# A PSUM bank per tile and chunk from a table, 32x32 score tiles, and a new hand-written order of all steps, in an attention and FP4 feed-forward block

## The chip, the cores and the metric

The kernel runs on one core of a Trainium2 chip. Its engines are TensorE (PE, with its weight loads listed apart as PEld), VectorE (DVE), ScalarE (ACT), GpSimd (POOL) and SyncE (SP, which issues transfers). The metric is the device time of one execution in microseconds, the median of several.

## The reference, cut to what matters

A sequence of 2048 tokens of width 128 goes through a retention layer with 8 heads (16 wide for q and k, 32 for v), then a gated feed-forward layer (352 wide) whose inputs and weights are rounded blockwise to FP4. Each of the two is followed by a residual sum and a layer norm.

```python
q, k, v = x @ Wq, x @ Wk, x @ Wv            # q and k are rotated (rope)
decay  = where(diff >= 0, exp2(diff * s[head]), 0)
scores = einsum('bhqd,bhkd,hqk->bhqk', q * DQK ** -0.5, k, decay)
o = einsum('bhqk,bhkd->bhqd', scores, v)
o = o * rsqrt(mean(o * o) + EPS) * g_norm_w * silu(x @ Wg)
x = layernorm(x + o @ Wo)
h = silu(fp4_linear(x, w_gate)) * fp4_linear(x, w_up)
x = layernorm(x + fp4_linear(h, w_down))
```

`fp4_linear` divides each block of 16 by a sixth of its largest absolute value, rounds to the FP4 grid, scales back, and multiplies.

## The kernel before, in words

The tokens are worked through in 16 chunks of 128 (`C`), each of two half chunks of 64 (`CH`). All matmuls are in float32. A matmul of the program is two passes on TensorE (a transpose is one), so `scores` with 8 matmuls has 16 records a chunk. The retention runs over half chunks: a state `S` carries what came before, and a masked product of q and k covers the half chunk itself.

The steps of one chunk, by engine:

- PE: `project_qk`, `project_vg`, `transpose_qk`, `state_product` (k times v, tile `U`), `scores` (k times q, tile `sc`), `from_state` (q times S, opens tile `oT`), `values` (adds probs times v to `oT`), `transpose_o`, `transpose_y`, `out_projection` (tile `att`), `transpose_xq`, `gate`, `up`, `transpose_h`, `down`.
- DVE: `rotate` (rope products), `mask_scores`, `next_state` twice, `mean_square`, `gated`, `ln1_eps`, five steps of quantization of x and five of h (`amax`, `inv`, `ratio`, `plus`, `grid`), `h_product`, `ln2_sum`.
- ACT: the copies out of PSUM, SiLU, squares for the norms, the norms themselves, and `magic` of the quantization.
- POOL: `rotate_add`, reciprocal roots (`rms_rstd`, `ln1_rstd`, `ln2_rstd`), `gated_output`, `x_value`, `h_value`.

Before chunk 0 is through, the feed-forward weights are quantized too (`weights_...` on DVE and ACT) and transposed on PE.

Each engine has its own list of calls, written out by hand for the whole kernel, and works it off in that order; the engines meet in semaphores. The lists are a software pipeline: near the middle, PE works on `scores(8)`, `out_projection(6)`, `gate(4)` and `project_qk(12)` in one stretch.

PSUM has 8 banks. A table `BANKS` gives each kind of tile one bank (`sc` and `oT` four, `U` two), the same for all chunks. Before a step of PE writes a bank, `occupy` calls `free`, which waits until the reader of that bank's last tile is done. In the kernel before, it waits for as many readings as tiles of that kind have been filled.

The scores of one chunk are 8 matmuls: 4 pairs of heads, each in its own 32 rows of the array, times 2 half chunks of 64 keys, each in its own 64 columns of the array. In `from_state` a matmul takes 32 rows and 32 columns, in `state_product` and `values` 64 rows and 32 columns.

Of the kernel before, what the change touches and what calls it, by code (L numbers as in the profile page):

```python
# [7 lines left out]
H = 128  # L8
NH = 8
DQK = H // NH  # L10
VD = 2 * H
DV = VD // NH
I = 352
IP = 384
C = 128
# [59 lines left out]
def seq_postln_kernel(nc, x, xt, wqk, wvg, wo_g, w_gate_up, w_down, tab, cst, out):  # L75
# [4 lines left out]
    with ExitStack() as ctx:  # L80
# [3 lines left out]
        def sem(name):  # L84
# [79 lines left out]
        bank = lambda name: ps[:, BANKS[name][0], :]  # L164
        sc_ps = lambda j: ps[:, BANKS["sc"][j], 0:C]
        all_sc_ps = ps[:, 0:4, 0:C]
        oT_ps = ps[:, 0:4, 0:CH]
        oT_bank = lambda half, a: ps[:, BANKS["oT"][2 * half + a], 0:CH]
        o_ps = bank("o")[:, 0:VD]
        yT_ps = bank("yT")[:, 0:VD]  # L170
        qk_ps = bank("qk")[:, 0:256]
        qkT_ps = bank("qkT")[:, 0:256]
        vg_ps = bank("vg")[:, :]
        att_ps = bank("att")[:, 0:H]
        gate_ps = bank("gate")[:, 0:I]
        xqT_ps = bank("xqT")[:, 0:C]
        hT_ps = bank("hT")[:, 0:384]
        up_ps = bank("up")[:, 0:I]
        down_ps = bank("down")[:, 0:H]
        U_ps = lambda a: ps[:, BANKS["U"][a], 0:2 * DV]  # L180
        wg_T_ps, wu_T_ps = ps[:, 3, 0:I], ps[:, 2, 0:I]
        wd_T_ps = ps[:, 5, 0:384]
# [62 lines left out]
        def _(pe_engine):  # L245
# [5 lines left out]

            def free(n):
                name = tile.get(n)
                if name == "sc":
                    pe.wait_ge(mask_v, filled[name])
                elif name == "qk":
                    pe.wait_ge(rope_v, filled[name])
                elif name == "qkT":
                    pe.wait_ge(qe_act, filled[name])
                    pe.wait_ge(kT_act, filled[name])  # L260
                    pe.wait_ge(qo_act, filled[name])
                elif name == "vg":
                    pe.wait_ge(v_act, filled[name])
                    pe.wait_ge(silu_g_act, filled[name])
                elif name == "oT":
                    pe.wait_ge(oT_act, filled[name])
                elif name == "o":
                    pe.wait_ge(gate_v, filled[name])
# [671 lines left out]
```

## Time and profile before

| | |
|---|---|
| median of 3 runs | 133.45 us (133.18 to 134.6) |
| the profiled execution | 132.9 us, of which its span, first to last instruction, is 131.2 us |
| mean granted TensorE clock | 0.992 |
| busy | PE 119.2 us, DVE 110.0, ACT 88.8, POOL 87.7 |

The page gives busy time from first start to last end of each instruction, and matmuls overlap in the pipeline. What a PE step costs the next one is therefore better read from the distance between their starts in the timeline.

### The profile page before, as it was taken

Reading aid. Unit: us, or ns where it says so; the run is one execution under the profiler, and the core shown is the slowest. Engines: PE = TensorE matmul, PEld = TensorE weight load, DVE = VectorE, ACT = ScalarE, POOL = GpSimd, SP = SyncE. Lnnn points to the kernel's source line nnn. Section 1 sums busy time; section 2 is a strip of 40 time slices with the busy share of each in tenths; the row PEclk is TensorE's granted clock in tenths of the full one; section 3 lists DMA queues with packets and bytes.
Section 4 is the critical chain, followed back from the end, with each engine's and each line's share of the span. In section 5 each row is a group of like instructions: output and inputs, shape, how many; then the busy total and the mean of one; then the engine's idle time right before and its main releaser. Section 6 shows DMA issues by size and latency. Waiting matters only on the chain.

```text
span 131.2 us, 5084 instructions
## 1 busy us (share of the span) xinstructions
PE 119.2 (91%) x2040; PEld 82.7 (63%) x2040; DVE 110.0 (84%) x329; ACT 88.8 (68%) x311; POOL 87.7 (67%) x124
## 2 busy tenths in 40 slices
PE   4859699989999999999999999899999999999860
PEld 4425257766667676766675576567696788887650
DVE  1249999689589999999999998899999999999810
ACT  3143847557674776839576858778696878898882
POOL 5202726577687849784783869476949797996781
PEclk9999999999999999999999999999999999999996
DMA  3899991000000000000000000000000000011222
GB/s 104 256 273 392 425 440 45 5 5 5 0 5 0 5 0 5 0 7 0 5 2 5 0 5 2 5 0 5 0 5 0 25 2 0 20 40 30 58 80 80
DMA packets 4791, 7.68 MB, mean 59 GB/s; under 512 B 800, under 2 KB 3872, under 8 KB 4512
## 3 DMA queue, kind: packets, MB, share of 16 engines
q1 hardware_dynamic: 3744, 6.60, 14.3%
q10 hardware_dynamic: 1024, 0.76, 1.8%
q8 instruction: 16, 0.26, 0.9%
q14 instruction: 7, 0.06, 0.2%
HBM read 6.31 MB, written 1.05 MB: 56 GB/s over the span
## 4 chain that ended last, share of the span: by engine, by line
PE 66%; DVE 16%; DMA 6%; issue 4%; ACT 3%; POOL 2%; SPq 1%; POOLq 0%; DVEq 0%
PE ps L313 7%; PE ps L441 7%; DMA tabs_sb<-rope_tables 6%; PE ps L421 6%; PE ps L427 6%; PE ps L330 5%; PE ps L307 4%; PE ps L355 4%; PE ps L365 4%; DVE probs L727 3%; PE ps L433 3%; PE ps L386 3%; PE ps L341 3%; PE ps L388 2%; PE ps L387 2%
## 5 line engine op out<-in xcount | busy, mean ns | idle before, releaser
L859 POOL TENSOR_TENSOR rstd_h<-ms,minus_half 128x8 f32<-128x8 f32 x16 | 26.8, 1672 | 6.9 <-DVE ms L743 6.8
L313 PE MATMUL ps<-w_vg,xT_sb 128*128 128x512 f32 x32 | 17.4, 625 | 1.5 <-DVE S L738 1.1
L854 POOL TENSOR_TENSOR qk<-rope 128x256 f32<-128x256 f32 x16 | 11.7, 729 | 9.7 <-DVE rope L721 9.7
L878 POOL TENSOR_TENSOR xq<-x_ratio,xs 128x128 f32<-128x128 f32 x16 | 7.8, 489 | 11.9 <-DVE x_ratio L656 11.9
L441 PE MATMUL ps<-wd_T,hT 128*128 128x128 f32 x96 | 14.1, 283 | 1.3 <-DVE r L757 0.7
L721 DVE TENSOR_TENSOR rope<-ps,tabs_sb 128x512 f32<-128x512 f32 x16 | 11.0, 687 | 4.6 <-DMA tabs_sb<-rope_tables 3.3
L870 POOL TENSOR_TENSOR rstd<-veps,minus_half 128x1 f32<-128x1 f32 x16 | 9.3, 579 | 7.7 <-DVE veps L752 7.7
L886 POOL TENSOR_TENSOR hq<-h_ratio,hs 128x352 f32<-128x352 f32 x16 | 13.0, 815 | 1.7 <-DVE h_ratio L656 1.4
L441 PEld LDWEIGHTS ps<-wd_T,hT 128*128 128x128 f32 x96 | 12.1, 191 | 3.1 <-ACT hT L483 1.5
L727 DVE TENSOR_TENSOR probs<-ps,causal 128x512 f32<-128x512 f32 x16 | 11.0, 690 | 2.8 <-PE ps L330 2.4
L421 PE MATMUL ps<-wgu_T,xqT 128*128 128x352 f32 x32 | 13.3, 496 | 0.0
L483 ACT ACTIVATE oT<-ps 128x256 f32<-128x256 f32 x16 | 6.1, 382 | 9.9 <-PE ps L365 9.8
L427 PE MATMUL ps<-wgu_T,xqT 128*128 128x352 f32 x32 | 12.2, 464 | 0.0
L307 PE MATMUL ps<-w_qk,xT_sb 128*128 128x256 f32 x32 | 10.8, 421 | 1.0 <-DMA xT_sb<-x_transposed 1.0
L864 POOL TENSOR_TENSOR y<-gate_o,rstd_h 128x256 f32<-128x256 f32 x16 | 10.4, 651 | 0.5
L484 ACT ACTIVATE q_eo<-ps,consts 128x128 f32<-128x128 f32 x32 | 10.7, 376 | 0.0
L738 DVE SCALAR_TENSOR_TENSOR S<-S,consts,ps 128x64 f32<-128x64 f32 x31 | 8.3, 269 | 2.6 <-PE ps L341 2.2
L874 POOL TENSOR_TENSOR rstd<-veps,minus_half 128x1 f32<-128x1 f32 x16 | 9.1, 579 | 1.5 <-ACT r_sq L580 1.5
L483 ACT ACTIVATE v_sb<-ps 128x256 f32<-128x256 f32 x16 | 6.3, 391 | 5.0 <-PE ps L313 5.0
L561 ACT ACTIVATE silu_h<-ps 128x352 f32<-128x352 f32 x16 | 7.4, 463 | 2.8 <-PE ps L421 2.5
L501 ACT ACTIVATE h_magic<-h_ratio 128x352 bf16<-128x352 f32 x16 | 7.9, 496 | 1.5 <-DVE h_ratio L647 1.4
L483 ACT ACTIVATE hT<-ps 128x384 f32<-128x384 f32 x16 | 7.8, 487 | 1.6 <-PE ps L433 1.6
(110 smaller groups left out, 340.1 us busy)
## 6 DMA issues: line engine op xcount, KB each, us to landing
tabs_sb<-rope_tables SPq DMA_DIRECT2D x1, 2048.0 KB, 12.0
tabs_sb<-rope_tables SPq DMA_DIRECT2D x1, 1280.0 KB, 8.1
out<-x SPq DMA_DIRECT2D x16, 64.0 KB, 1.5
tabs_sb<-rope_tables SPq DMA_DIRECT2D x1, 512.0 KB, 4.6
xT_sb<-x_transposed SPq DMA_DIRECT2D x1, 512.0 KB, 7.6
xT_sb<-x_transposed SPq DMA_DIRECT2D x1, 320.0 KB, 5.5
tabs_sb<-rope_tables SPq DMA_DIRECT2D x1, 256.0 KB, 3.6
w_vg<-in_w_vg ACTq DMA_DIRECT2D x1, 256.0 KB, 3.9
```

Of the source, the lines that this page charges most:

```text
L307: mm(qk_ps, xT(c), w_qk[:], start=True, stop=True).then_inc(qk_pe, 1)
L313: mm(vg_ps, xT(c), w_vg[:], start=True, stop=True).then_inc(vg_pe, 1)
L421: mm(gate_ps, xqT[:, c % D, :], wgu_T[:, 0:I], start=True, stop=True).then_inc(gate_pe, 1)
L427: mm(up_ps, xqT[:, c % D, :], wgu_T[:, I:2 * I], start=True, stop=True).then_inc(up_pe, 1)
L441: last = mm(down_ps, hT[:, c % D, t, :], wd_T[:, t, :], start=t == 0, stop=t == 2)
L483: copy = lambda o, i: nc.scalar.activation(o, i, ACT.Copy)
L484: scaled = lambda o, i, by: nc.scalar.activation(o, i, ACT.Identity, scale=by)
L721: vec.tensor_tensor(rope[:, c % D, :, :], qk_ps.unsqueeze(1).to_broadcast([128, 2, 256]), tabs(c).rearrange("p (t n) -> p t n", t=2), ALU. ...
L727: vec.tensor_tensor(probs[:, c % D, :, :].rearrange("p (j e) q -> p j e q", e=2), all_sc_ps.rearrange("p j (e q) -> p j e q", e=2), causal ...
L854: gp.tensor_tensor(g16(qk[:, c % D, :]), g16(rope[:, c % D, 0, :]), g16(rope[:, c % D, 1, :])[:, :, ::-1, :], ALU.add).then_inc(qk_p, 1)
L859: gp.tensor_tensor(rstd_h[:, c, :], ms[:, c, :], minus_half[:], ALU.pow).then_inc(rms_p, 1)
L886: gp.tensor_tensor(hq[:, c % D, 0:I].rearrange("p (n k) -> p n k", k=BLK), h_ratio[:, c % 6, :].rearrange("p (n k) -> p n k", k=BLK), hs[: ...
```

## The change

1. Banks. `BANKS` now has an entry for each kind and chunk, so that for example `down` uses banks 7, 7, 3, 7, 5, ... instead of always 6. `sc` and `oT` keep banks 0 to 3 in every chunk. Each bank remembers which tile, and which count of it, it holds, and `free` waits for that count alone.
2. Scores. The 8 matmuls of 32 rows by 64 columns become 16 of 32 by 32 with the same 128 moving columns each.
3. Orders. The lists of PE, ACT, DVE and POOL are all rewritten. The calls are the same, but for a second `warm_up(4)` on PE (4 matmuls on an identity) between `project_qk(0)` and `project_vg(0)`. Most calls move by less than four places.
4. One added wait: `h_ratio_` of chunk 6 and later waits on DVE for `h_value` of six chunks before, which is the last reader of the buffer it writes.

```diff
-        BANKS = {"sc": (0, 1, 2, 3), "oT": (0, 1, 2, 3), "o": (1,), "yT": (7,), "qk": (4,), "qkT": (0,),
-                 "vg": (6,), "att": (5,), "xqT": (2,), "gate": (4,), "hT": (3,), "up": (7,),
-                 "down": (6,), "U": (6, 7)}
+        BANKS = {
+            "sc": (0, 0, 0, 0, 0, 0, 0, 0, 0, 0, 0, 0, 0, 0, 0, 0),
+            "oT": (0, 0, 0, 0, 0, 0, 0, 0, 0, 0, 0, 0, 0, 0, 0, 0),
+            "o": (2, 1, 1, 3, 3, 0, 2, 3, 2, 0, 0, 1, 0, 2, 1, 3),
+            "yT": (3, 4, 7, 6, 3, 3, 0, 0, 2, 7, 4, 4, 3, 4, 6, 6),
+            "qk": (5, 6, 6, 4, 6, 4, 4, 4, 4, 4, 4, 4, 4, 1, 4, 2),
+            "qkT": (2, 3, 2, 3, 2, 0, 2, 1, 2, 1, 3, 3, 3, 2, 0, 4),
+            "vg": (4, 4, 7, 5, 7, 6, 4, 6, 6, 6, 6, 6, 6, 6, 6, 6),
+            "att": (5, 5, 5, 5, 5, 5, 5, 5, 5, 5, 5, 5, 5, 5, 4, 0),
+            "xqT": (5, 6, 1, 5, 1, 5, 4, 6, 4, 4, 4, 6, 6, 6, 6, 6),
+            "gate": (4, 4, 4, 4, 4, 4, 4, 4, 4, 4, 4, 4, 2, 5, 5, 5),
+            "hT": (7, 7, 4, 0, 0, 1, 3, 7, 4, 7, 0, 3, 2, 3, 7, 7),
+            "up": (7, 7, 7, 7, 7, 7, 4, 7, 1, 1, 2, 6, 1, 2, 2, 2),
+            "down": (7, 7, 3, 7, 5, 7, 1, 7, 3, 4, 6, 5, 0, 5, 3, 3),
...
+            def banks(name, c):
+                b = BANKS[name][c]
+                return b if name == "U" else range(b, b + BANKS_OF.get(name, 1))
...
             def occupy(name, banks):
+                filled[name] += 1
                 for n in banks:
                     free(n)
-                    tile[n] = name
-                filled[name] += 1
+                    tile[n] = name, filled[name]
...
-                for a in range(2):
+                for k in range(4):
                     for j in range(NP):
-                        rows, keys = slice(32 * j, 32 * j + 32), slice(CH * a, CH * a + CH)
-                        last = mm(sc_ps(j)[keys, :], kT[rows, c % D, keys],
-                                  q_eo[rows, c % D, a, :, :].rearrange("p e q -> p (e q)"), start=True, stop=True)
+                        rows, keys = slice(32 * j, 32 * j + 32), slice(32 * k, 32 * k + 32)
+                        last = mm(sc_ps(c, j)[keys, :], kT[rows, c % D, keys],
+                                  q_eo[rows, c % D, k // 2, :, :].rearrange("p e q -> p (e q)"), start=True, stop=True)
...
-            def h_ratio_(c): quant_ratio(h(c), sh(c), blocks(h_ratio[:, c % 6, :]), hquant_v, c)
+            def h_ratio_(c):
+                if c >= 6:
+                    dve.wait_ge(hq_p, c - 5)
+                quant_ratio(h(c), sh(c), blocks(h_ratio[:, c % 6, :]), hquant_v, c)
```

The head of the orders of PE and DVE, before and after:

```diff
-            warm_up(4); project_qk(0); project_vg(0); transpose_qk(0); project_qk(1); state_product(0); scores(0)
-            project_vg(1); from_state(0); values(0); state_product(1); project_qk(2); transpose_qk(1); transpose_o(0)
+            warm_up(4); project_qk(0); warm_up(4); project_vg(0); transpose_qk(0); state_product(0); scores(0)
+            project_vg(1); project_qk(1); from_state(0); values(0); project_qk(2); transpose_o(0); state_product(1)
...
-            rotate(0); weights_amax(0); next_state(0, 0); next_state(0, 1); rotate(1); mask_scores(0); weights_inv(0)
-            weights_amax(1); weights_ratio(0); next_state(1, 0); rotate(2); next_state(1, 1); mean_square(0)
+            rotate(0); weights_amax(0); next_state(0, 0); weights_inv(0); next_state(0, 1); mask_scores(0)
+            weights_ratio(0); rotate(1); weights_amax(1); weights_inv(1); rotate(2); next_state(1, 0); mean_square(0)
```

A stretch of PE's order in the middle, and the end of the orders of PE and DVE:

```diff
-            out_projection(6); from_state(8); state_product(9); values(8); gate(4); transpose_qk(9); transpose_o(8)
-            transpose_y(7); project_vg(10); project_qk(12); transpose_xq(5); up(4); scores(9); out_projection(7)
+            transpose_xq(4); up(3); scores(8); out_projection(6); from_state(8); state_product(9); values(8); gate(4)
+            transpose_o(8); transpose_qk(9); project_vg(10); transpose_y(7); project_qk(12); up(4); transpose_xq(5)
+            scores(9); out_projection(7); from_state(9); state_product(10); values(9); gate(5); transpose_o(9)
...
-            transpose_xq(14); down(7); gate(14); transpose_h(9); up(14); down(8); transpose_h(10); transpose_xq(15)
-            down(9); up(15); gate(15); transpose_h(11); down(10); transpose_h(12); down(11); transpose_h(13); down(12)
+            down(6); transpose_h(8); transpose_xq(14); down(7); gate(14); up(14); down(8); transpose_h(9)
+            transpose_xq(15); transpose_h(10); gate(15); down(9); up(15); transpose_h(11); down(10); transpose_h(12)
...
-            h_plus_(13); h_ratio_(14); ln2_sum(9); h_grid_(13); h_plus_(14); h_product(15); ln2_sum(10); h_grid_(14)
-            h_amax(15); ln2_sum(11); h_inv(15); h_ratio_(15); ln2_sum(12); h_plus_(15); h_grid_(15); ln2_sum(13)
+            h_inv(14); h_plus_(13); h_ratio_(14); h_grid_(13); ln2_sum(9); h_plus_(14); h_product(15); h_amax(15)
+            h_inv(15); ln2_sum(10); h_grid_(14); h_ratio_(15); ln2_sum(11); h_plus_(15); h_grid_(15); ln2_sum(12)
```

## Rows read from the trace of the kernel before

**Rows 1.** The page: busy time by engine; PE's busy tenths in 40 slices.

```profile
PE 119.2 (91%) x2040; PEld 82.7 (63%) x2040; DVE 110.0 (84%) x329; ACT 88.8 (68%) x311; POOL 87.7 (67%) x124
...
PE   4859699989999999999999999899999999999860
```

**Rows 2.** Busy time by engine in windows of 10 us.

```profile
0.00:10.00 10.00, 6.27 (x49) 3.82 (x50) 2.92 (x12) 2.92 (x7) 2.45 (x13) 1.00 0.72 214
10.00:20.00 10.00, 8.57 (x184) 4.74 (x185) 9.93 (x24) 5.73 (x17) 3.78 (x4) 1.00 1.02 413
...
50.00:60.00 10.00, 9.87 (x226) 6.98 (x226) 9.62 (x31) 6.01 (x24) 7.74 (x10) 1.00 0.02 4
```

**Rows 3.** Timeline of the head (start, length, idle before and who ended it).

```profile
1.85 2.08 PE L301 MATMUL ps<-ident 128*128 128x128 f32 x8 [1.85 <-POOL ident L838]
...
5.18 1.63 PE L313 MATMUL ps<-w_vg,xT_sb 128*128 128x512 f32 x2 [0.40 <-DMA w_vg<-in_w_vg]
...
6.88 0.89 DVE L639 TENSOR_REDUCE wr_small<-wgu_nat 128x44 f32<-128x704 f32 x1 [1.29 <-DMA wgu_nat<-in_w_gate_up]
...
8.95 0.47 PE L330 MATMUL ps<-q_eo,kT 32*64 32x128 f32 x16
9.24 0.60 DVE L738 SCALAR_TENSOR_TENSOR S<-S,consts,ps 128x64 f32<-128x64 f32 x2 [1.48 <-PE ps L341]
...
9.85 0.69 DVE L721 TENSOR_TENSOR rope<-ps,tabs_sb 128x512 f32<-128x512 f32 x1
...
10.46 0.68 DVE L727 TENSOR_TENSOR probs<-ps,causal 128x512 f32<-128x512 f32 x1
...
11.05 0.33 DVE L673 TENSOR_SCALAR wr_small<-wr_small 128x44 f32<-128x44 f32 x1
...
11.80 0.51 DVE L639 TENSOR_REDUCE wr_small<-wd_nat 128x22 f32<-128x352 f32 x1
```

**Rows 4.** Timeline of PE in the middle: scores, output projection, from_state, state product.

```profile
38.40 0.48 PE L330 MATMUL ps<-q_eo,kT 32*64 32x128 f32 x16
38.80 0.49 PE L386 MATMUL ps<-centring,xT_sb 128*128 128x128 f32 x2
39.13 0.39 PE L387 MATMUL ps<-wo_c,yT 128*128 128x128 f32 x2
39.35 0.39 PE L388 MATMUL ps<-wo_c,yT 128*128 128x128 f32 x2
39.72 0.46 PE L355 MATMUL ps<-q_eo,S 32*32 32x64 f32 x32
40.10 0.34 PE L341 MATMUL ps<-v_sb,qk 64*32 64x64 f32 x16
...
40.76 0.56 PE L421 MATMUL ps<-wgu_T,xqT 128*128 128x352 f32 x1
```

**Rows 5.** The list of waits (us in total, times, longest).

```profile
PEld ps L355 <- DVE probs L727: 4.3, 11, 0.9
...
PE ps L313 <- DVE S L738: 1.1, 2, 0.7
...
PE ps L441 <- DVE r L757: 0.7, 2, 0.5
...
PE ps L330 <- DVE gate_o L748: 0.6, 2, 0.4
```

**Rows 6.** Timeline late in the kernel: h_value(6) on POOL, h_ratio(12) on DVE.

```profile
103.01 0.89 POOL L886 TENSOR_TENSOR hq<-h_ratio,hs 128x352 f32<-128x352 f32 x1 [0.38 <-PE ps L433]
...
109.01 0.52 DVE L647 SCALAR_TENSOR_TENSOR h_ratio<-h_blocks,hs 128x352 f32<-128x352 f32 x1
```

**Rows 7.** Timeline of the tail: gate(15), h_product(15), down(14).

```profile
118.46 0.75 PE L421 MATMUL ps<-wgu_T,xqT 128*128 128x352 f32 x2
...
119.81 0.53 DVE L775 TENSOR_TENSOR h_blocks<-ps,silu_h 128x352 f32<-128x352 f32 x1
...
124.65 0.91 PE L441 MATMUL ps<-wd_T,hT 128*128 128x128 f32 x6 [0.48 <-DVE r L757]
```

More of the change, by code:

```diff
@@ L465, in _ @@
-            state_product(12); values(11); gate(7); transpose_qk(12); transpose_o(11); transpose_y(10); project_vg(13)
-            project_qk(15); up(7); transpose_xq(8); out_projection(10); scores(12); gate(8); from_state(12)
-            values(12); state_product(13); transpose_o(12); transpose_qk(13); transpose_y(11); project_vg(14)
-            transpose_xq(9); up(8); scores(13); out_projection(11); from_state(13); state_product(14); values(13)
-            gate(9); transpose_o(13); transpose_qk(14); transpose_h(0); transpose_y(12); project_vg(15); up(9)
@@ new lines, in _ @@
+            out_projection(1); project_qk(6); scores(3); state_product(4); from_state(3); values(3); project_qk(7)
+            transpose_o(3); transpose_qk(4); transpose_xq(0); project_vg(5); transpose_y(2); gate(0); scores(4)
+            out_projection(2); from_state(4); values(4); state_product(5); project_qk(8); transpose_o(4)
+            transpose_qk(5); transpose_y(3); up(0); project_vg(6); scores(5); transpose_xq(1); out_projection(3)
+            from_state(5); state_product(6); values(5); gate(1); transpose_o(5); transpose_y(4); transpose_qk(6)
@@ new lines, in _ @@
+            from_state(11); state_product(12); values(11); gate(7); project_qk(15); transpose_qk(12); transpose_o(11)
+            up(7); transpose_y(10); project_vg(13); transpose_xq(8); scores(12); out_projection(10); gate(8)
+            from_state(12); values(12); state_product(13); transpose_y(11); transpose_o(12); transpose_qk(13); up(8)
+            project_vg(14); scores(13); transpose_xq(9); out_projection(11); from_state(13); state_product(14)
+            values(13); gate(9); transpose_o(13); up(9); transpose_y(12); transpose_qk(14); project_vg(15)
@@ new lines, in _ @@
+            transpose_xq(10); transpose_h(0); scores(14); out_projection(12); gate(10); from_state(14); values(14)
+            state_product(15); transpose_y(13); transpose_o(14); up(10); transpose_h(1); transpose_qk(15)
+            out_projection(13); transpose_xq(11); down(0); scores(15); gate(11); up(11); from_state(15); values(15)
+            transpose_h(2); transpose_y(14); transpose_o(15); transpose_h(3); down(1); transpose_xq(12)
+            out_projection(14); gate(12); up(12); transpose_h(4); down(2); transpose_y(15); down(3); transpose_h(5)
@@ L829, in _ @@
+            ln2_sum(7); x_plus_(15); h_inv(13); x_grid_(15); h_ratio_(13); h_product(14); h_amax(14); ln2_sum(8)
+            h_inv(14); h_plus_(13); h_ratio_(14); h_grid_(13); ln2_sum(9); h_plus_(14); h_product(15); h_amax(15)
+            h_inv(15); ln2_sum(10); h_grid_(14); h_ratio_(15); ln2_sum(11); h_plus_(15); h_grid_(15); ln2_sum(12)
+            ln2_sum(13); ln2_sum(14); ln2_sum(15)
         @block.gpsimd
```

398 lines of the change are left out of this document (194 added, 204 removed).

## Prediction

> **What bounds the kernel now.** I read the page first. PE is busy for 91% of the span, DVE for 84%, and PE's slices are full from about 30 us to 123 us [rows 1]. The windows of 10 us say more: from 10 to 20 us DVE is the full engine (9.93 of 10) while PE has 8.57; in the middle (50 to 60 us) both are nearly full, PE with 9.87 and DVE with 9.62; in the first 10 us PE has 6.27 and DVE only 2.92 [rows 2]. So there are two engines that can't lose much, a head in which both idle, and a tail of about 8 us after PE's last full slice that is one chain of steps of chunk 15.
>
> Busy time of PE is not yet work, since matmuls overlap. In the timeline of the middle the starts are what counts: two passes of 128 columns stand 0.22 us apart (39.13 to 39.35), which is 0.11 us a pass, and the next group follows without a hole, save where the array changes from full to small tiles (39.35 to 39.72 is 0.37, so 0.15 us over the streaming) [rows 4]. PE is thus bound by its own stream there, and waits for banks are rare: the list of waits has 1.1 us for `U`'s reader (bank 6, both times in the head), 0.6 us for `gated` (bank 1 ahead of `scores`) and 0.7 us for `ln2_sum` (bank 6 ahead of `down`) [rows 5].
>
> **The sum is made part by part, against the profiled 132.9 us (span 131.2 us and 1.7 us around it).** The median of the runs, 133.45 us, is 0.55 us above it; I add that at the end.
>
> **1. The head.** Before, DVE finishes `weights_amax(0)` at 7.77 (6.88 and 0.89) and idles 1.48 us until `state_product(0)` is through (9.24), since PE has `project_qk(1)` ahead of it, which waits for its input. Then `rotate(1)` stands at 9.85, after its table's transfer, and only then come `mask_scores(0)` at 10.46 and `weights_inv(0)` from 11.05 to 11.80 [rows 3]. From here to 20 us DVE is full, so what it has done by 9.85 is what it gains. The new order puts `state_product(0)` and `scores(0)` on PE ahead of `project_qk(1)`, and on DVE `weights_inv(0)` into the idle 1.48 us and `mask_scores(0)` and `weights_ratio(0)` ahead of `rotate(1)`. `weights_inv(0)` is 0.75 us (11.05 to 11.80), and it fits whole. What more is gained is part of `mask_scores(0)` (0.68 us), if scores are there in time; PE could start them some 0.6 us earlier than 8.95. At most the whole idle 1.48 us is filled. I take -1.0 us, between 0.75 and 1.48 and nearer the first.
>
> Against it stands the second `warm_up(4)`. The first one has 8 passes in 2.08 us, 0.26 us a pass. It goes between `project_qk(0)` and `project_vg(0)`, where PE waits for the weights until 5.18. If its 8 passes take 0.11 us each, as in the middle [rows 4], they hide; at 0.26 us they end some 1.2 us after 5.18, and `project_vg(0)`, which took 1.63 us from 5.18, is late, with the copies of ACT and `transpose_qk(0)` queued behind it [rows 3]. The time it gives back is that a later matmul might run at the shorter pass: 4 times 256 columns are 8 passes, 0.88 us against the 1.63. So the delay behind `project_vg(0)` is between none and about 0.5 us, and the part ends between -1.5 and +0.2 us.
>
> **2. Banks in the middle.** The largest wait behind a bank, 4.3 us of weight loads of `from_state` that wait for `mask_scores` (11 times), stays, because `sc` and `oT` keep banks 0 to 3 in every chunk [rows 5]. It shows only a little in PE's stream, as `out_projection` lies between. The 1.1 us behind `U` are in the head and counted there. Left are 0.6 us of `gated` and 0.7 us of `ln2_sum`, and `o` now moves over four banks and `down` over seven. But `scores` takes all of banks 0 to 3 and so still waits for every `o`, `qkT`, `yT` or `hT` that was put there; new such waits replace some of the old. Also DVE has only 0.4 us of idle in 10 in the middle [rows 2], so PE cannot run away from it: what the banks could give is capped by DVE. I take -0.5 us, and -1.5 to +1.0 us as bounds.
>
> **3. The other moves.** Most calls move by two or three places between neighbours of the same pipeline stage; the stretch from `scores(8)` to `scores(9)` has the same 13 calls on PE before and after. They cost nothing as long as the tile that a step needs is done a step earlier. `out_projection`, 0.59 us from 39.13 back to 38.80 and on to 39.72, still stands between `scores` and `from_state` and covers the 0.68 us of `mask_scores` in part [rows 3, 4]. I count zero and keep the +1.0 us of part 2 as what it costs if a reader is late.
>
> **4. The added wait of h_ratio.** `h_ratio_(12)` waits for `h_value(6)`. Before, that one ended at 103.90 and `h_ratio_(12)` started at 109.01, 5.1 us later; it is the closest of the ten pairs [rows 6]. A wait that is met costs nothing; behind it on DVE would be `h_plus_` and all later steps of the tail. Zero.
>
> **5. Scores in 32x32 tiles.** 16 passes of 128 columns become 32, so PE executes 256 more in the kernel (2040 now [rows 1]), besides 8 of the warm-up. Before, the 16 passes take 0.40 us from their first start to the next step's (38.40 to 38.80). A pass of 128 columns streams in 0.11 us, and 16 in turn would be 1.76 us, so small tiles run side by side. The nearest row for 32 passes in 32x32 tiles is `from_state`: 0.38 us (39.72 to 40.10) with 64 columns, 0.055 us of streaming a pass. With 128 columns the last pass ends 0.055 us later: 0.44 us, which is 0.035 us more than 0.40, or +0.6 us in 16 chunks. Next row: `state_product` and `values` in 64x32 tiles have 48 passes in 0.66 us (40.10 to 40.76), 0.014 us each; 32 of them are 0.44 us, and 0.055 us more is 0.49, or +1.5 us in all. From below: 16 tiles at once would need two passes (0.22 us) and the 0.15 us of the change of tiles, 0.37 us, or -0.5 us in all. I take +0.6 us, for `from_state` has the very tile shape [rows 4].
>
> What the Trainium skill says against it: "Each matmul has ~60 cycle overhead on TRN2" (TensorEngine Tiling (Array Packing), Instruction Overhead), which at 2.4 GHz is an estimate of 0.025 us, so that 16 more passes a chunk would cost 0.4 us, and 6.4 us in 16 chunks. The trace disagrees: the 32 passes of `from_state` take 0.38 us in all, 0.012 us each [rows 4].
>
> **6. The tail.** Before, `gate(15)` is the last of chunk 15's two products (118.46), and `h_product(15)` starts at 119.81, after SiLU; now `gate(15)` goes first, and SiLU runs under `down(9)` and `up(15)`. `h_amax(15)` follows `h_product(15)` at once, without `ln2_sum(10)` and `h_grid_(14)` between. `down(14)` waited 0.48 us for `ln2_sum(13)` to free bank 6; it now has another bank [rows 7]. These overlap: the chain ends with chunk 15's `h_value`, transposes and `down`, so the wait of `down(14)` is worth only the part that delays `transpose_h(15)`. I take -0.45 us, between 0 and -0.9.
>
> Sum: -1.0 - 0.5 + 0 + 0 + 0.6 - 0.45 = -1.35 us. 132.9 - 1.35 = 131.55; with the 0.55 us to the median, 132.1 us, 1.0% below 133.45. About 1% is also what a measurement of this kernel can tell from no change.
>
> **The rivals.**
>
> *Given back (about 133.4 us).* DVE is nearly full from 30 us on, so the lead from the head and the banks is lost where DVE's list binds: the head's 1.0 us ends in a longer wait of DVE for PE near 25 to 30 us, and `scores` adds its 0.6 us. For it: DVE's 9.62 in 10. Against: from 10 to 20 us DVE is itself the full engine, and it starts earlier. Time: 133.45 - 0.45 (tail) + 0.6 - 0.2 = 133.4 us.
>
> *Scores serialize in their rows (about 139 us).* The mechanism for slower: passes in the same 32 rows of the array can't stream side by side in different columns. Then 8 passes share each row group, 8 times 0.11 is 0.88 us against the 4 times 0.11 = 0.44 us before, which fits the 0.40 us seen. Price: 0.88 - 0.40 = 0.48 us a chunk, 7.7 us in all, on PE, which is full. 133.45 - 1.95 (the gains of parts 1, 2 and 6) + 7.7 = 139.2 us. It decides from the point where a group takes more than 1.95 / 16 = 0.12 us longer, 0.52 us. Against it: `from_state` has 8 passes a row group too, 8 times 0.055 = 0.44 us, and took 0.38 us with the change of tiles included [rows 4]. That is a narrow margin, so it keeps a chance.
>
> *The banks don't do what they say (about 134.9 us).* `scores` needs four banks free at once, and now up to four different readers (`gated`, `copy_yT`, `q_even` and the others, `copy_hT`) stand behind them. If each of 10 middle chunks waits 0.25 us more, which is less than the longest such wait of 0.4 us [rows 5], that is +2.5 us: 132.1 + 2.5 + the lost 0.5 of part 2 is 135.1; with half of the tail's gain kept, 134.9 us.
>
> **Chances.** Forecast, a gain of 0.5 to 4 us: 0.52, of which 0.46 is over 1%, since all parts at their favourable ends give -1.5 - 1.5 - 0.5 - 0.9 = -4.4 us and the middle gives 1%. Given back: 0.26. Serialized scores: 0.09. New bank waits: 0.13. Of the forecast's and the given-back case's 0.78, 0.32 are within 1%, to which 0.02 of the bank case come: 0.34. Slower by over 1%: 0.20. The range that leaves out no more than 2 in 10 reaches down to 129.6 us (the favourable ends are rarely all met; 0.07 below) and up to 135.2 us (the bank case in, the serialized case out; 0.12 above). For the forecast alone it is 129.6 to 132.8 us.
>
> **What the profile of the changed kernel would show.** Scores: 32 records from first to next step's start within 0.38 to 0.49 us; 0.88 us would show the serialized case. Head: DVE without the 1.48 us hole before 9.24, and the first weights' transposes about 1 us earlier. Warm-up: `project_vg(0)` shorter than 1.63 us. Banks: the waits of `down` for `ln2_sum` gone, and no new waits of `scores` for `copy_yT` or `copy_hT`. Tail: `h_product(15)` less than 1.35 us after `gate(15)`'s start plus the 0.66 us of the `down` between them. The prediction is wrong if DVE's list, and not PE's stream, sets the middle's pace, or if one group of small tiles costs other than its nearest row.

## The result, and the profile after

The changed kernel takes 135.38 us in the median of 20 runs, the kernel before 133.81 us beside it: a ratio of 1.0112, with a 95% interval of 1.0077 to 1.0147. It is 1.1% slower, where a gain of 1.0% was forecast. The profile shown here is of a second launch of the same kernel (134.96 us, ratio 1.011, interval 1.008 to 1.014), since in the execution profiled first TensorE's granted clock fell to 0.50 for 3.4 us, from 93.4 us on.

The page of the changed kernel: span, busy time by engine, PE in 40 slices, and the queue that brings an engine its instructions (transfers, MB, share).

```profile
span 133.2 us, 5629 instructions
...
PE 119.3 (90%) x2304; PEld 83.5 (63%) x2304; DVE 112.0 (84%) x329; ACT 89.4 (67%) x311; POOL 88.1 (66%) x124
...
PE   4979899989999999999997969795999999999960
...
q8 instruction: 18, 0.29, 0.9%
```

PE is busy for 119.3 us, as before, in a span that is 2.0 us longer. Its slices were full from 30 to 123 us [rows 1]; now four notches (7, 6, 7, 5) stand in them between 70 and 93 us. The last row is one that I hadn't read: 18 transfers of instructions, where before there were 16 with 0.26 MB. The windows of 10 us of the changed kernel (span, then PE, PEld, DVE, ACT, POOL with their instructions, granted clock, DMA) put the loss in the same place:

```profile
60.00:70.00 10.00, 9.73 (x247) 6.52 (x245) 9.54 (x29) 7.17 (x26) 7.15 (x9) 1.00 0.02 4
70.00:80.00 10.00, 8.00 (x175) 5.41 (x157) 9.07 (x26) 5.28 (x19) 5.92 (x10) 1.00 0.01 2
80.00:90.00 10.00, 9.20 (x231) 5.62 (x230) 8.67 (x29) 7.19 (x26) 6.24 (x8) 1.00 0.02 4
90.00:100.00 10.00, 8.57 (x182) 5.81 (x173) 8.75 (x28) 7.02 (x24) 5.92 (x9) 1.00 0.01 3
```

All engines fall together there, at a granted clock of 1.00, which is 2.4 GHz. The timeline of PE in that stretch of the changed kernel shows what stands still. `values` is one step of 32 passes; it is cut in two each time, and what ended the idle time before its second half isn't a semaphore ("issue"):

```profile
69.80 0.54 PE L383 MATMUL ps<-probs,v_sb 64*32 64x64 f32 x27
...
71.21 0.31 PE L383 MATMUL ps<-probs,v_sb 64*32 64x64 f32 x5 [0.87 <-issue]
...
76.26 0.46 PE L383 MATMUL ps<-probs,v_sb 64*32 64x64 f32 x20
...
77.81 0.33 PE L383 MATMUL ps<-probs,v_sb 64*32 64x64 f32 x11 [1.09 <-issue]
...
83.78 0.44 PE L383 MATMUL ps<-probs,v_sb 64*32 64x64 f32 x28
...
85.02 0.30 PE L383 MATMUL ps<-probs,v_sb 64*32 64x64 f32 x4 [0.80 <-issue]
...
89.80 0.28 PE L383 MATMUL ps<-probs,v_sb 64*32 64x64 f32 x7
...
91.52 0.43 PE L383 MATMUL ps<-probs,v_sb 64*32 64x64 f32 x25 [1.43 <-issue]
```

The list of waits of the changed kernel (us in total, times, longest) has them as one row, the largest of PE's own:

```profile
PE ps L383 <- issue: 4.2, 4, 1.4
...
PE ps L459 <- ACT hT L501: 0.8, 2, 0.6
...
PE ps L373 <- DVE probs L745: 0.4, 1, 0.4
```

**What the four places have in common.** I numbered all records of PE and PEld in the order of their starts, the waits for semaphores among them, and set beside them the transfers of queue q8. Each transfer has 16,384 bytes. The changed kernel has 4717 such records, 4608 loads and passes and 109 others, and 18 transfers (before 4186, of which 4080 are loads and passes, and 16 transfers). The changed kernel's four holes lie behind the records 3009, 3265, 3521 and 3777, exactly 256 apart, and so does a small one in its head. For each such end, worked out from the records (times in us):

```
changed kernel
end of    its next block's    records left   started in       crossed   hole   after transfer's
block     transfer starts     at that time                    at               start
 449      13.92               112            the head         16.25     0.34   2.32
1985      44.04               217            out_projection   49.03     0.00   4.99
2241      50.00               203            out_projection   55.09     0.01   5.09
2497      56.09               188            out_projection   60.31     0.13   4.22
2753      61.95               178            out_projection   64.58     0.00   2.63
3009      68.38               157            out_projection   71.21     1.08   2.83
3265      75.05               146            out_projection   77.81     1.31   2.76
3521      82.42               127            out_projection   85.02     1.01   2.60
3777      89.21               112            out_projection   91.52     1.65   2.31
4033      93.15               194            transpose_y      97.58     0.00   4.43
kernel before
1985      51.49               220            out_projection   56.52     0.06   5.02
2241      57.66               237            out_projection   63.34     0.00   5.68
2497      63.69               254            out_projection   70.44     0.00   6.76
2753      70.10               267            gate             76.06     0.00   5.96
3009      76.44               198            state_product    82.60     0.00   6.16
3265      83.40               140            state_product    88.23     0.00   4.83
3521      89.21               162            gate             94.50     0.00   5.29
3777      95.52               165            down            101.16     0.00   5.64
```

At the holes PE goes on 2.3 to 2.8 us after the transfer begins. The transfers themselves take 0.9 to 1.4 us in this trace, and from a transfer's end it is 1.27 to 1.49 us to the record behind the hole. No trace of this case has an earlier crossing: over all 13 kept traces there are 208 block ends with a transfer, and none is crossed sooner than 1.22 us after that transfer has ended. In the changed kernel the transfers start in the same step ten times on end, `out_projection`, 266 to 277 records apart, while the blocks end 256 apart. So the records left at a start shrink by some 15 a chunk, from 244 to 112. A chunk in the middle has some 272 records there, the waits counted. Before, it had 240, and the number left rose (220, 237, 254, 267). And behind `out_projection` come the densest steps, `from_state` (64 records of both kinds), `state_product` (32) and `values` (64), each some 0.4 us: PE is through the last 157 to 112 records, of which the last 152 to 112 are such steps without a break, in 1.7 to 0.7 us, where before 140 to 165 of them, with large steps between, took 4.8 us and more. Together the four holes are 5.05 us. This was the theory after the result (theory A, supply of instructions); its rivals were that a group of 32x32 tiles costs more time by itself, and that the new banks or orders do.

The Trainium skill has this mechanism, and I hadn't looked there: instructions are "refilled in 16 KiB blocks (256 instructions)" (Runtime: NRT & Kernel Launch, Instruction fetch mechanics). The trace agrees with this size: 16,384 bytes a transfer, and holes 256 records apart. The Trainium skill also calls crossing a block's end "mostly hidden"; here four crossings of 18 cost 1.01 to 1.65 us each.

### The profile page after: what moved, and what is told of

Its sections match the earlier page's. It is cut to its first block, busy times and chain, and to the rows that moved or that the text cites. A ratio compares the mean times of both kernels' runs of the same rounds, so it can differ in the third digit from the quotient of the medians.

```text
span 136.1 us, 5629 instructions
## 1 busy us (share of the span) xinstructions
PE 122.3 (90%) x2304; PEld 85.3 (63%) x2304; DVE 111.7 (82%) x329; ACT 89.7 (66%) x311; POOL 88.3 (65%) x124
## 3 DMA queue, kind: packets, MB, share of 16 engines
q1 hardware_dynamic: 3744, 6.60, 14.1%
## 4 chain that ended last, share of the span: by engine, by line
PE 59%; DVE 25%; issue 6%; ACT 5%; DMA 2%; POOLq 0%; POOL 0%; DVEq 0%
PE ps L331 9%; PE ps L439 6%; PE ps L348 5%; PE ps L325 5%; PE ps L445 5%; PE ps L383 4%; PE ps L373 4%; DVE probs L745 3%; PE ps L359 3%; PE ps L404 3%; DMA w_qk<-in_w_qk 2%; DVE hs L657 2%; DVE h_blocks L793 2%; DVE h_ratio L674 2%; DVE h_ratio L665 2%
## 5 line engine op out<-in xcount | busy, mean ns | idle before, releaser
L891 POOL TENSOR_TENSOR rstd<-veps,minus_half 128x1 f32<-128x1 f32 x16 | 9.6, 599 | 8.7 <-DVE veps L770 8.7
L439 PE MATMUL ps<-wgu_T,xqT 128*128 128x352 f32 x32 | 13.4, 501 | 0.0
L501 ACT ACTIVATE oT<-ps 128x256 f32<-128x256 f32 x16 | 6.1, 381 | 10.9 <-PE ps L383 10.9
L383 PE MATMUL ps<-probs,v_sb 64*32 64x64 f32 x512 | 9.4, 222 | 4.2 <-issue 4.2
L445 PE MATMUL ps<-wgu_T,xqT 128*128 128x352 f32 x32 | 12.7, 481 | 0.0
L895 POOL TENSOR_TENSOR rstd<-veps,minus_half 128x1 f32<-128x1 f32 x16 | 9.7, 617 | 1.2 <-ACT r_sq L598 1.2
L383 PEld LDWEIGHTS ps<-probs,v_sb 64*32 64x32 f32 x512 | 6.6, 105 | 5.6 <-issue 4.8
L348 PE MATMUL ps<-q_eo,kT 32*32 32x128 f32 x512 | 8.4, 279 | 1.1 <-ACT q_eo L502 0.5
```

Of the source, the lines that this page charges most:

```text
L348: last = mm(sc_ps(c, j)[keys, :], kT[rows, c % D, keys], q_eo[rows, c % D, k // 2, :, :].rearrange("p e q -> p (e q)"), start=True, stop=True)
L383: last = mm(oT_bank(c, n // 4, a)[32 * slot32:32 * slot32 + 32, :], v_sb[keys, c % D, n * DV:(n + 1) * DV], probs[keys, c % D, n, :], star ...
L439: mm(gate_ps(c), xqT[:, c % D, :], wgu_T[:, 0:I], start=True, stop=True).then_inc(gate_pe, 1)
L445: mm(up_ps(c), xqT[:, c % D, :], wgu_T[:, I:2 * I], start=True, stop=True).then_inc(up_pe, 1)
L501: copy = lambda o, i: nc.scalar.activation(o, i, ACT.Copy)
```

## The experiments

Each ratio is to the kernel before, run beside it on the same chip; its medians there were 133.48, 133.4 and 133.44 us.

**1. The change without its small tiles** (`a_sc64`), new banks and orders kept:

```diff
-                for k in range(4):
+                w = 64
+                for k in range(C // w):
...
-                        rows, keys = slice(32 * j, 32 * j + 32), slice(32 * k, 32 * k + 32)
+                        rows, keys = slice(32 * j, 32 * j + 32), slice(w * k, w * k + w)
```

> The changed kernel with its scores back in 32x64 tiles (8 matmuls, 16 passes a chunk); banks and orders stay new. Theory A: TensorE runs out of instructions. Its stream comes in blocks of 256, the four holes of 1.03 to 1.65 us inside values stand exactly 256 records apart (3009, 3265, 3521, 3777), and the 512 extra instructions of the small score tiles made a chunk about as long as a block, so that the block's end fell into the dense small-tile steps chunk after chunk. Then the holes vanish here, and the time falls by their 5.0 us, less what was hidden: 129.5 to 131.5 us, 2 to 3% below before. Theory B: the new orders and banks are themselves the cost and the tiles cost only their 0.04 us a chunk: 134.5 to 135.5 us, and holes or new semaphore waits remain.

Measured: 130.47 us, 0.9775 (0.9727 to 0.9823). Its page, of the same views as above:

```profile
span 128.7 us, 5117 instructions
...
PE 118.9 (92%) x2048; PEld 83.5 (65%) x2048; DVE 110.6 (86%) x329; ACT 89.4 (69%) x311; POOL 88.4 (69%) x124
...
PE   4979989989999999999999999999999999999960
...
q8 instruction: 16, 0.26, 0.9%
```

PE has the same 119 us of work, but in a span 4.5 us shorter, and there are no notches. Two more rows of its windows say the same of the stretch in question:

```profile
70.00:80.00 10.00, 9.99 (x163) 6.14 (x151) 10.00 (x32) 7.32 (x25) 7.27 (x11) 1.00 0.01 2
80.00:90.00 10.00, 9.71 (x214) 6.33 (x213) 9.67 (x33) 7.89 (x28) 6.32 (x10) 1.00 0.01 3
```

Here the ends behind records 3009 to 3777 are crossed 4.5 to 6.5 us after their transfers start (with 256, 152, 140 and 152 records left). They lie in `from_state`, so inside the dense steps too, but only 24 to 61 records into them, where at the holes it is 112 to 152; the rest of what was left at the start are large steps. So banks, orders and the second warm-up together bring a good 2%, and the small tiles take away over 3%.

**2. The small tiles alone, on the kernel before** (`b_sc32`): the loop of the change's diff, with the banks and orders of before.

> The kernel before with nothing changed but its scores in 32x32 tiles. Theory A: the stream grows from 16 to 18 blocks and each block's end falls elsewhere; holes of about 1 us without a semaphore appear in scores, from_state or values of some chunks. 134 to 139 us by how many blocks end there; the scores themselves stay within 0.38 to 0.49 us a chunk. Theory B (the tile shape costs only its few hundredths of a microsecond): 133.8 to 134.6 us, no holes. Third theory (32x32 passes are slow in themselves): scores take over 0.5 us from first to next start in every chunk.

Measured: 135.92 us, 1.0179 (1.0127 to 1.0231), span 134.3 us. The timeline of PE has one cut of the kind in it:

```profile
89.96 0.40 PE L366 MATMUL ps<-probs,v_sb 64*32 64x64 f32 x18
...
91.40 0.34 PE L366 MATMUL ps<-probs,v_sb 64*32 64x64 f32 x14 [1.04 <-issue]
```

It lies at the same block end, 3777, with the transfer's start at 89.07, 2.33 us before 91.40 and 4.28 us after the previous block's end, which was crossed at 84.79. The small tiles cost 2.4 us here by the ratio, and a single large hole is 1.25 us of it; 0.6 us are the tiles' own time (below). The remaining half microsecond I can't place. The profiled spans are 3.1 us apart (134.3 and 131.2), and 1.0 us of that arises before `scores(5)` (39.4 against 38.4 us): in this execution TensorE's clock rose at 10.4 us, in the profiled one of the kernel before at 6.2 us (see 6).

**3. Large tiles in the first 2, 4 or 8 chunks only** (`a_sc64_first2`, `a_sc64_first4`, `a_sc64_first8`). These tell supply from price. If a small tile costs time by itself, each chunk made large again must help, and 8 more than 4. If block ends decide, what counts is where they fall: 8 chunks of large tiles take out 8 times 32 records, exactly one block, so the ends after chunk 8 fall on the same steps as in the changed kernel.

```diff
-                w = 64
+                w = 64 if c < 4 else 32
```

> The changed kernel with 32x64 score tiles in chunks 0 to 3 alone. The stream before chunk 4 is 128 instructions shorter, half a block, while the code of chunks 4 to 15, where the holes were, is word for word the same. Theory A: the block's ends move by 128 instructions to another place of the chunk, outside values; the four holes there go or move, any hole left stands at the same distance of 256 records. 130 to 134 us. Theory B, or anything that lies in the code of those chunks: the holes in values of chunks 10 to 13 stay, 135 us.

> The changed kernel with 32x64 score tiles in chunks 0 to 7, so the stream before chunk 8 is 256 instructions shorter: exactly one block, and the ends of blocks fall on the same instructions of chunks 8 to 15 as in the changed kernel. Theory A: the holes in values of chunks 10 to 13 are back, on the same passes, though fewer small score tiles are in the kernel than with first4, which had none: 133.5 to 135 us. Rival (holes come with the number of small-tile instructions): fewer or no holes, 131 to 131.5 us, between first4 (0.988 of before) and all 32x64 (0.978).

> The changed kernel with 32x64 score tiles in chunks 0 and 1 alone: the stream before chunk 2 is 64 instructions shorter, so each block's end falls 64 instructions later in the code than in the changed kernel, out of values and into the full-size steps behind it. Theory A: the same number of small tiles as in the changed kernel but for two chunks, and yet no hole of 1 us in values of chunks 10 to 13; a shorter one may stand right behind. 130.8 to 132.5 us. Rival (number of instructions alone): still three or four holes, 134 to 135 us.

| chunks with 32x64 tiles | ratio (interval) | median, us | profiled span, us | holes in `values(10)` to `values(13)` |
|---|---|---|---|---|
| none (the change) | 1.011 (1.008 to 1.014) | 134.96 | 133.2 | 1.08, 1.31, 1.01, 1.65 |
| first 2 | 0.9929 (0.9889 to 0.9969) | 132.76 | 131.4 | none (one of 1.03 in `state_product` of a later chunk) |
| first 4 | 0.9878 (0.9816 to 0.9941) | 131.78 | 129.7 | none |
| first 8 | 1.0042 (0.9998 to 1.0085) | 134.25 | 132.2 | 0.54, 1.31, 1.01, 1.37 |
| all 16 | 0.9775 (0.9727 to 0.9823) | 130.47 | 128.7 | none |

Twice as many large tiles as in `a_sc64_first4` make the kernel 1.7% slower (1.0042 over 0.9878). The timeline of PE of `a_sc64_first8` has the cuts of the changed kernel again, behind the passes 20, 28 and 7 of `values`:

```profile
75.49 0.45 PE L384 MATMUL ps<-probs,v_sb 64*32 64x64 f32 x20
...
77.03 0.33 PE L384 MATMUL ps<-probs,v_sb 64*32 64x64 f32 x11 [1.09 <-issue]
...
83.01 0.44 PE L384 MATMUL ps<-probs,v_sb 64*32 64x64 f32 x28
...
84.24 0.30 PE L384 MATMUL ps<-probs,v_sb 64*32 64x64 f32 x4 [0.80 <-issue]
...
89.02 0.29 PE L384 MATMUL ps<-probs,v_sb 64*32 64x64 f32 x7
...
90.47 0.43 PE L384 MATMUL ps<-probs,v_sb 64*32 64x64 f32 x25 [1.16 <-issue]
```

In `a_sc64_first2`, whose 132.76 us are a little above the 132.5 us expected, the ends lie 64 records away, and PE's timeline shows the large hole in another dense step, again 2.39 us after a transfer's start (93.73):

```profile
94.97 0.33 PE L360 MATMUL ps<-v_sb,qk 64*32 64x64 f32 x12
...
96.12 0.30 PE L360 MATMUL ps<-v_sb,qk 64*32 64x64 f32 x4 [0.82 <-issue]
```

**4. The change without the second warm-up** (`a_nowarm2`). It takes 8 passes and 8 loads out ahead of everything else, so every block end should move 16 records, 8 passes, further into the steps.

```diff
-            warm_up(4); project_qk(0); warm_up(4); project_vg(0); transpose_qk(0); state_product(0); scores(0)
+            warm_up(4); project_qk(0); project_vg(0); transpose_qk(0); state_product(0); scores(0)
```

> The changed kernel without its second warm_up(4). The stream is 16 instructions shorter, so by theory A each hole comes 16 instructions (8 passes) later in the code: in values of chunk 10 and 12, where it was 4 to 8 passes before the end, it may just leave the step, and in those of 11 and 13 it stays, later in the step. Also shows what the warm-up costs in the head: project_vg(0) started at 6.72 us with it and 5.18 without, so the head should run up to 1 us earlier. 133 to 135.4 us. Theory B: the holes stay on the same pass of values.

Measured: 136.31 us, 1.0208 (1.0139 to 1.0278), span 134.4 us, above the range expected. PE's timeline:

```profile
78.22 0.54 PE L383 MATMUL ps<-probs,v_sb 64*32 64x64 f32 x28
...
79.77 0.30 PE L383 MATMUL ps<-probs,v_sb 64*32 64x64 f32 x3 [1.01 <-issue]
...
91.23 0.32 PE L383 MATMUL ps<-probs,v_sb 64*32 64x64 f32 x15
...
92.75 0.35 PE L383 MATMUL ps<-probs,v_sb 64*32 64x64 f32 x17 [1.21 <-issue]
```

The cuts stand behind passes 28 and 15, where they stood behind 20 and 7: 8 passes on, as the block size asks. At the other two ends, which have moved past the last pass of `values`, 0.35 and 0.22 us are left of 1.08 and 1.01. That ties the holes to the place in the stream of instructions, and to nothing that the step computes. The holes are 3.2 us now instead of 5.05, and still the kernel is not faster (1.0208 against 1.0112, with intervals that overlap a little). The reason is in the head: `scores(5)` starts at 39.6 us, and at 36.7 in the changed kernel. The runs of 6 are about that.

**5. The changed kernel again** (`after_again`), without an edit, and **the new orders with the old banks** (`a_sc64_oldbanks`), large tiles in all chunks, the bank table and the fixed banks of warm-up and weights as before:

```diff
-        BANKS = {
-            "sc": (0, 0, 0, 0, 0, 0, 0, 0, 0, 0, 0, 0, 0, 0, 0, 0),
...
+        BANKS = {n: (b,) * NC for n, b in {"sc": 0, "oT": 0, "o": 1, "yT": 7, "qk": 4, "qkT": 0, "vg": 6, "att": 5,
+                                           "xqT": 2, "gate": 4, "hT": 3, "up": 7, "down": 6, "U": (6, 7)}.items()}
```

> The changed kernel once more, unchanged, for a second profile beside the next ones. Theory A (ends of instruction blocks): four holes inside values of chunks 10 to 13, again at records 256 apart and within a pass or two of where they were. Rival (chance, such as memory traffic of others): the holes stand elsewhere or are missing. 134.5 to 135.5 us.

> New orders, scores in 32x64, but the old bank for every kind of tile in all chunks. Tells the banks' share of the 0.978 that new orders and new banks reach together. If the banks give it: 132.5 to 133.5 us, with waits of scores for gated, of project_vg for the state and of down for ln2_sum back. If the orders and the warm-up give it: 130.5 to 131.5 us. The new order was written for the new banks, so a longer time than before is possible too, by waits of transpose_y for project_vg's readers and the like.

The first is the profile shown above; the four holes are there as expected, and in the execution profiled first too, behind the same four records. The second is far outside what was expected: a median of 158.12 us, and a ratio of 1.1651 (1.1597 to 1.1705) that rests on two executions of 155.17 and 155.62 us. Of its list of waits:

```profile
PE ps L383 <- DVE S L743: 3.0, 3, 1.2
...
PE ps L432 <- ACT yT L488: 2.9, 5, 1.3
...
PE ps L383 <- DVE h_blocks L780: 2.6, 2, 1.4
...
PE ps L346 <- ACT silu_g L541: 2.5, 3, 1.4
```

PE waits for readers of a bank (`yT`, `silu_g`, `h_blocks`) in step after step. The new order needs its banks. The reverse, the old orders with the new table, wasn't run. By the code it would lock up: the table puts `qk` of chunk 1 and `U` of chunk 0 both in bank 6, so `state_product(0)` would wait for `rotate(1)`, which on the old DVE list stands behind `next_state(0, 0)`, and that waits for `state_product(0)`. So the gains of the two aren't told apart here, and what another table would be worth on the old order stays untried.

**6. The second warm-up.** Three kernels: large tiles without it (`a_sc64_nowarm2`), large tiles with half of it (`a_sc64_warm2`, `warm_up(2)`), and the kernel before with it and nothing else (`b_warm2nd`):

```diff
-            warm_up(4); project_qk(0); project_vg(0); transpose_qk(0); project_qk(1); state_product(0); scores(0)
+            warm_up(4); project_qk(0); warm_up(4); project_vg(0); transpose_qk(0); project_qk(1); state_product(0); scores(0)
```

> New orders and banks, scores in 32x64, without the second warm_up(4). The same comparison as a_nowarm2 with the changed kernel (1.021 against 1.011 of before), but free of the holes. If the warm-up itself was worth about 1%, this one takes 131.5 to 132 us and project_vg(1) runs its 512 columns at 1.0 us a pass instead of 0.43; if it was the holes' change of place, 130.5 us as with the warm-up.

> New orders and banks, scores in 32x64, the second warm-up with 2 matmuls instead of 4. project_vg(0) could start when its weights land (5.2 to 5.7 us) instead of 6.28. If the four passes less still bring the shorter passes before 8 us, the head is up to 0.8 us earlier: 129.7 us, 0.972 of before. If not, project_vg(1) runs at 0.85 to 1.0 us a pass and the time goes to that of no second warm-up, 132.5 us.

> The kernel before with nothing but the second warm_up(4) added. Prediction's part 1 had a delay of 0 to 0.5 us for it. If in the old order project_vg(0) simply starts later and the head waits for the tables' transfer at 9.8 us anyway, nothing changes: 133.2 to 134.0 us. If longer passes in the first 12 us cost the kernel before something in most executions, it falls to 132 to 132.5 us.

Measured: 132.54 us without it (7 runs, 132.26 to 132.96 and one of 129.4; no interval, so this comparison is not settled), against 130.47 with it; 130.53 us, 0.9752 (0.969 to 0.9814), with half of it; and 132.85 us, 0.9921 (0.9879 to 0.9962), for the kernel before with it. The first lies a little above the 131.5 to 132 us expected, and the second between the two outcomes expected. The timeline of PE of `a_sc64_nowarm2`:

```profile
5.66 2.07 PE L331 MATMUL ps<-w_vg,xT_sb 128*128 128x512 f32 x2 [0.79 <-DMA w_vg<-in_w_vg]
...
9.95 2.08 PE L331 MATMUL ps<-w_vg,xT_sb 128*128 128x512 f32 x2
```

and of `a_sc64_warm2`:

```profile
5.43 1.23 PE L331 MATMUL ps<-w_vg,xT_sb 128*128 128x512 f32 x2
...
8.65 1.12 PE L331 MATMUL ps<-w_vg,xT_sb 128*128 128x512 f32 x2
```

The same two passes take 2.07 us without and 1.23 us with it, and it is the same in chunk 1, 4 us later. In the kernel before, the row of `project_vg(0)` has 1.63 us [rows 3]; with the warm-up alone it has 1.02.

The windows print a granted clock of 1.00 for these stretches in either case. But the trace's own list of granted clocks has no entry there: its first one, at full speed (2.4 GHz), begins at 14.5 us in `a_sc64_nowarm2` and 14.1 in `a_nowarm2`, at 5.7 in `a_sc64_warm2`, 6.9 in `a_sc64` and 5.2 in the changed kernel, and the windows take what has no entry for 1.00. The passes change at the same moment: in the changed kernel's second warm-up they start 0.21 us apart until 5.2 us and 0.11 us apart from there. So ahead of the first entry TensorE worked at half that speed, which is the level of 1.2 GHz; this is worked out from the distances, as no entry names it. In the changed kernel PE had worked without a pause from 1.85 us up to the rise; in `a_sc64_nowarm2` it stood still for 0.79 us ahead of 5.66. What the added matmuls buy is an earlier rise. When it comes differs between executions of the same calls: 5.2 and 8.0 us in the two profiles of the changed kernel, 6.2 and 10.4 us in those of the kernel before and `b_sc32`, whose calls are the same up to `scores(0)`. The one execution of `a_sc64_nowarm2` with 129.4 us may have had an early rise; it wasn't profiled.

So a few matmuls in a place where PE only waits for its weights gave 0.8% on the old order, neither of the two outcomes expected there. Of the 19 executions of the kernel before beside it, eight took 134.2 to 135.6 us and eleven 132.8 to 133.5; the ten with the warm-up all took 132.6 to 133.3 us. On the new order the medians are 2 us apart, with the reservation above.

## Why the prediction was wrong

**The step that failed is part 5, scores in 32x32 tiles.** It took +0.6 us, and up to +1.5, from the distance of starts in the array. For the array that holds: from the first start of `scores` to the next step's is 0.463 us in the mean of the changed kernel and 0.426 in `a_sc64`, 0.04 us a chunk where 0.035 was said. What it left out, and so put at nothing, is the supply of instructions: PE gets 512 more of them, two more blocks, of the densest kind. A chunk then has some 272 instructions, more than the 256 of a block, where before it had 240, fewer; so the lead of the supply shrank from chunk to chunk instead of growing, until the ends fell into `values` four chunks in a row. The part cost 4.6 us (1.0112 over 0.9775). The four holes are 5.05 us and the tiles' own time 0.6 us; 1.1 us or so of the two together was won back elsewhere, which I didn't follow up. None of my rivals for this part was right: the rows don't serialize (32 passes in 0.43 to 0.47 us in 14 of 16 chunks, never 0.88), and the overhead that the Trainium skill gives a matmul isn't to be seen. To reach 4.6 us, the 256 added passes would have had to cost 0.018 us each, but the loss sits nearly all in four places.

**Part 1, the head: right, and somewhat small.** `scores(5)` starts at 37.1 us in `a_sc64`, at 38.4 before: -1.3 us where -1.0 was taken. In these two profiles the clock rose at 6.9 and 6.2 us, so an earlier rise isn't part of it. The timelines of the changed kernel show the steps. PE first:

```profile
5.76 1.02 PE L331 MATMUL ps<-w_vg,xT_sb 128*128 128x512 f32 x2
...
8.14 0.51 PE L348 MATMUL ps<-q_eo,kT 32*32 32x128 f32 x32 [0.54 <-ACT q_eo L502]
8.59 1.13 PE L331 MATMUL ps<-w_vg,xT_sb 128*128 128x512 f32 x2
```

and DVE:

```profile
6.84 0.89 DVE L657 TENSOR_REDUCE wr_small<-wgu_nat 128x44 f32<-128x704 f32 x1 [1.13 <-DMA wgu_nat<-in_w_gate_up]
7.81 0.28 DVE L756 SCALAR_TENSOR_TENSOR S<-S,consts,ps 128x64 f32<-128x64 f32 x1
8.22 0.43 DVE L693 RECIPROCAL wr_small<-wr_small 128x44 f32<-128x44 f32 x1
...
8.89 0.69 DVE L745 TENSOR_TENSOR probs<-ps,causal 128x512 f32<-128x512 f32 x1
9.50 0.88 DVE L665 SCALAR_TENSOR_TENSOR wr_ratio<-wgu_nat,wr_small 128x704 f32<-128x704 f32 x1
```

The 1.48 us hole of DVE is gone, `scores(0)` starts 0.81 us and `mask_scores(0)` 1.57 us earlier than before [rows 3]. The second warm-up was set down as a cost of up to 0.5 us with a vague return; it delays `project_vg(0)` by 0.58 us (5.76 against 5.18), which then takes 1.02 us instead of 1.63. Its return wasn't seen for what it is: by the medians 0.8% on the old order (0.4 to 1.2%), and by the traces through an earlier rise of the clock, not through one shorter step.

**Part 2, banks in the middle, with part 3: right in size.** Between `scores(5)` and `scores(15)` another 0.4 us is gained (97.3 against 99.0 us), where -0.5 was taken. The new waits that were feared don't come; behind the holes the list of the changed kernel has 1.8 us for the identity at the very start, as before, and then 0.8 us for `hT` as the next largest. But the reasoning was poor: the table isn't worth 0.5 us beside the order. With the old banks the new order is 16.5% slower than the kernel before. The rival with new bank waits also has a slip in its sum: half of the tail's gain was already in the 132.1 us, so keeping it can't lower 135.1 to 134.9 us.

**Part 4, the added wait:** DVE's list of waits has no row for POOL's `hq`, as said.

**Part 6, the tail: the size right to 0.4 us, one step wrong.** From `scores(15)` to the end of the span it is 31.4 us in `a_sc64` and 32.2 before, -0.8 where -0.45 was taken. `h_product(15)` starts 2.22 us after `gate(15)` there, more than the 2.01 us (1.35 and the `down`'s 0.66) that the prediction allowed, since it waits for `up(15)` too, which ends at 117.72. But from it to the end it is 10.9 us instead of 11.35, and no `down` waits for a bank any more; two still wait for `hT` (0.23 and 0.58 us). These three rows of PE and DVE in the tail of `a_sc64` are `gate(15)`, `h_product(15)` and two `down` in one piece:

```profile
115.59 0.86 PE L440 MATMUL ps<-wgu_T,xqT 128*128 128x352 f32 x2
...
117.81 0.52 DVE L794 TENSOR_TENSOR h_blocks<-ps,silu_h 128x352 f32<-128x352 f32 x1
...
121.39 1.70 PE L460 MATMUL ps<-wd_T,hT 128*128 128x128 f32 x12
```

**The sum.** Parts 1, 2, 3, 4 and 6 were -1.95 us and are -3.0 us by the runs (0.9775); part 5 was +0.6 and is +4.6. That makes 133.8 - 3.0 + 4.6 = 135.4 us. (The profiles alone show -1.3 - 0.4 - 0.8 = -2.5 us; the profiled execution of the kernel before was 0.9 us under the median.) The forecast's direction hung on part 5 alone, and the range's upper end of 135.2 us came from another case, new bank waits, that didn't occur. The best version is the change with its old tiles, with two or four matmuls in the second warm-up: 2.3 to 2.5% faster than before.

**What stays open.** What makes a transfer of instructions start when it does. In the middle of the kernel it mostly starts within 2 us of the crossing of the previous block's end, but ahead of the four large holes 3.8 to 4.6 us after it, and in `b_sc32` 4.3 us. A late start alone costs little: in `a_sc64_warm2` three transfers start 3.3 to 4.0 us after the crossing, and the distances at their ends are 0.30, 0.11 and 0.11 us. A late start with the dense steps right behind it makes a hole; what makes the start late stays open. The first of the four starts ahead of the large holes follows an end that was crossed without a hole, 2.63 us after its transfer's start (64.58), so a block that is only just in time may delay the next; but 4033's transfer came 1.63 us after the largest hole. This, and why the starts keep to `out_projection`, wasn't tried. Nor was a version that keeps the small tiles and moves the dense steps off the block ends by a few added instructions, though the runs of 3 suggest a gain of 2% over the change (0.9878 against 1.011, with small tiles still in 12 chunks). And the price of small tiles without any hole isn't clean: `a_sc64_first4` has 12 chunks of them and is 1.4 us above `a_sc64`, 0.5 us of that as forecast, one hole of 0.45 us in the head, the rest not placed.

## What to carry to other kernels

Count instructions, and not only array time, when a step is split into smaller tiles: a float32 matmul is two loads and two passes here. Steps of many small ones used up 112 records in 0.66 us, 5.9 ns each; by that a block of 256 would last 1.5 us, an estimate, against the 2.2 to 2.9 us from a transfer's start to the first record behind a hole. If an engine stands still in the middle of a step with no semaphore behind it, number its records from the start of the kernel, waits included; when the breaks are 256 apart, it is the supply. A chunk of more than 256 instructions is a sign to look for (272 gave four large holes in one order and one in the other, 240 none in either), and moving a boundary by adding or removing a few instructions far ahead is a cheap test. A bank table and an order belong together: cost and test them as one. And where TensorE's first passes are twice as far apart as later ones, look at when its clock rises before anything else is compared in the head.

## What the runs showed of the hardware

- TensorE's instructions come in transfers of 16,384 bytes, and the holes stand 256 of its records apart, loads, passes and waits counted. The 15 holes of 1 us and more, in six traces, end 2.2 to 2.9 us after a transfer's start and 1.25 to 1.52 us after its end. None of the 208 block ends in the 13 traces is crossed earlier than 1.22 us after the transfer's end. Where the end came 3 us or more after the start, the distance to the next record was 0.41 us at most. No transfer started with more than 271 records left to the end of the block at work.
- Small tiles in all 16 chunks cost 3.4% with one placement of the block ends (the change against `a_sc64`), and in 12 of the 16 chunks 1% with another (`a_sc64_first4` against it).
- Passes of 512 columns took 1.04 us each (2.07 for two) until about 12 us where the second warm-up was missing, and 0.51 to 0.62 with it. The trace's first entry of a granted clock, at full speed, begins at 14.1 and 14.5 us without it and at 5.2 to 8.0 us with it on the new order; a granted clock of 1.00 in a window ahead of that entry says nothing.
